# Attention scores from two products over interleaved head rows in place of three, with the low parts moved by DMA

## The chip, the cores and the metric

The kernel runs on one core of one Trainium2 chip. The metric is the device time in microseconds (us) of one execution. The time before is 929.22 us, the median of three runs (926.53 to 930.88).

## The reference

Two cross-attention layers follow one another on 8192 tokens (32 batches of 256) with 320 channels, 20 heads of 16 channels each, and 77 context keys per batch. One layer is, in short:

```python
q = split_heads(x @ Wq)            # (32, 20, 256, 16)
k, v = split_heads(ctx @ Wk), split_heads(ctx @ Wv)   # (32, 20, 77, 16)
p = softmax(q @ k.T / 4)
x = merge_heads(p @ v) @ Wo + b + x
```

The second layer does the same to the output of the first, with its own weights. The object and image-prompt branches of the original have no keys here, so the text branch is all there is.

## The kernel before

**Tiling.** The work goes in 32 units `u` (`NU`), 16 for each layer. A unit is 512 tokens, which are two batches. Channels lie on the partitions in three blocks `m` of 128, 128 and 64 rows. A context unit `w` serves two units, so the projections of keys and values (`K`, `V` in the code) stand only in even units, which are therefore longer: an even and an odd unit together take about 55 us.

**Rounded products.** TensorE multiplies rounded operands (type F32R) fast, so a value is held as a rounded high part and a low remainder. Queries are `QH` and `QL`, keys `KH` and `KL`. A score is the sum of three products: `KH*QH`, `KH*QL` and `KL*QH`.

**Heads.** In a group of 32 rows lie two heads of 16 rows. The key tiles are masked, once for the first head and once for the second, so that a product over all 32 rows gives one head's scores. Four row groups `j` of 32 rows work on TensorE side by side.

**`run(u, k, n, ...)`** is the inner piece, called for k = 0 to 4 in each unit. In ten steps it issues the score matmuls of unit `u` (`keys_by_tokens`, L391), the subtraction of the row maxima (`less_maxima`, L397), and a rough set of scores of the next unit `n = u + 1` for those maxima (`tokens_by_keys`, L378). ScalarE then takes the exponential of the four PSUM banks (L763) and frees them for the next `run`. Between the runs stand, in an order written out by hand, the projections `Q`, `K`, `V` (L307, L257, L287), the output projection `out(u - 2)` (L307) and the product with the values `PV` (L444), which gives 16 output rows and one row of sums for each head. `take(..., bank, reader)` makes TensorE wait until the last reader of a PSUM bank is done; for a query projection of block m that reader is `Q_lo(u, m)`.

**VectorE** takes the maxima (L1034), makes the low parts (`Q_lo` L995, `K_lo` L958), copies PV's output from PSUM (`o_copy` L1049, writes `Oraw`), and adds bias and residual (L1101). Its order is written out by hand as well. At the end of an even unit it is: last maxima, `Q_lo(u+2, 2)`, `Q_hi(u+2, 1)` (L987), `Q_lo(u+2, 1)`, `split_o` (L1090), then `o_copy` of k = 4, 2, 3.

**SP** issues nearly all DMAs in one hand-made order, and a wait in it holds up everything that stands behind. For each unit these are: `load_x` (L1369, L1371; the second copies 64 rows into both halves of the partitions, `broadcast_to([2, 64, N])`), `values` (L1404), `sums` (L1417, L1422: the softmax sums into `Zg` and `Zt`), `natural` (L1434, L1441: 12 DMAs that merge PV's output into `On`), `put_recips` (L1448, L1451: the reciprocals to DRAM), `spread` (L1468: the reciprocals back from DRAM, each head's row repeated on 16 partitions), `store` (L1482, L1483) and, in even units, `load_c` (L1380). `load_x(u + 3)` waits until `store(u - 2)` has landed, since both use the same of five buffers `X32`. POOL multiplies `On` with the spread reciprocals (L1293) and splits it (L1300).

The order that SP follows in an even unit, after `put_recips`, is the line

```python
spread(v, 0); spread(v, 1); store(z); load_c(u // 2 + 2); sums(u, 0); load_x(u + 3)   # v = u - 1, z = u - 2
```

(written in one line here).

Of the kernel before, what the change touches and what calls it, by code (L numbers as in the profile page):

```python
# [7 lines left out]
F32 = mybir.dt.float32  # L8
# [8 lines left out]
N = 512  # L17
# [4 lines left out]
L4 = L * 4  # L22
MT = [128, 128, 64]
# [6 lines left out]
QC = 2 * N + SQ  # L30

# [3 lines left out]
def constants():  # L35
    ident = np.eye(128, dtype=np.float32)
    mask = np.zeros((128, 2), np.float32)
    for p in range(2):
        mask[(np.arange(128) // D) % 2 == p, p] = 1.0
    neg = np.zeros((128, NI), np.float32)  # L40
    for j in range(4):
        for i in range(NI):
            neg[32 * j + i, i] = -1.0
    return ident, mask, neg


def build(nc, a):
    with ExitStack() as ctx:
# [22 lines left out]
        KH = sb("KH", [128, 2, 4, 2, LK], F32R)  # L71
        KL = sb("KL", [128, 2, 4, 2, LK], F32R)
        KH2 = sb("KH2", [128, 4, LK], F32R)
        KL2 = sb("KL2", [128, 4, LK], F32R)
        Kt = sb("Kt", [128, L4])

        QH = sb("QH", [128, 2, QC], F32R)
        QL = sb("QL", [128, 2, QC], F32R)
# [3 lines left out]
        VA = sb("VA", [128, 2, 2, C + H])  # L82
# [15 lines left out]
        small = sb("small", [128, 4 * D])  # L98
        ones = small[0:L, :].rearrange("p (a d) -> p a d", a=2)
        Zt = small[96:128, :]  # L100
# [37 lines left out]
        d_va = [sem(f"d_va{i}") for i in range(2)]  # L138

# [35 lines left out]


# [26 lines left out]
        def _(pe):  # L203
# [140 lines left out]
            def run(u, k, n, first, second):  # L344
# [23 lines left out]
                if u is not None:  # L368
                    ms, p = GROUP[k]
                    if k % 2 == 0:  # L370
                        pe.wait_ge(q_lo[ms], u + 1)
                        pe.wait_ge(k_lo[ms], u // 2 + 1)

                def tokens_by_keys(t, j):

                    c0 = m * N + (b * 2 + t) * 128
                    kt = KH[32 * j:32 * j + 32, m, n % 4, b, :] if m < 2 else KH2[32 * j:32 * j + 32, n % 4, :]
                    return pe.matmul(pR[:, (second if j > 1 else first) + j % 2, t * LK:t * LK + LK],  # L378
# [3 lines left out]
                def keys_by_tokens(i, j):  # L382

                    h = i // 3
                    pp, c0 = (p, ms * N + h * SQ) if ms < 2 else (h, 2 * N)
                    Q_ = (QH, QL, QH)[i % 3]
                    if ms < 2:
                        kt = (KH, KH, KL)[i % 3][32 * j:32 * j + 32, ms, u % 4, h, :]
                    else:
                        kt = (KH2, KH2, KL2)[i % 3][32 * j:32 * j + 32, u % 4, :]  # L390
                    pe.matmul(pA[0:L, j, h * SQ:h * SQ + SQ], kt[:, pp * L:pp * L + L],  # L391
                              Q_[32 * j:32 * j + 32, u % 2, c0:c0 + SQ],
                              start=(i == 0), stop=False, skip_group_check=True)
# [6 lines left out]
                for step in range(10):  # L400
# [3 lines left out]
                    for j in (0, 1):  # L404
                        if step < 2 and n is not None:
                            f = tokens_by_keys(step, j)
                        if 2 <= step < 8 and u is not None:
                            keys_by_tokens(step - 2, j)
                        if step >= 8 and u is not None:
                            g = less_maxima(step - 8, j)  # L410
                    if n is not None and step == 1:
                        f.then_inc(x_pe, 1)
                    if u is not None and step == 9:
                        g.then_inc(s_pe, 1)

                    if n is not None and step == 8:
                        take_pair(second, 1)
                    for j in (2, 3):
                        if step < 6 and u is not None:
                            keys_by_tokens(step, j)  # L420
                        if 6 <= step < 8 and u is not None:
                            less_maxima(step - 6, j)
                        if step >= 8 and n is not None:
                            f = tokens_by_keys(step - 8, j)
                    if n is not None and step == 9:
                        f.then_inc(x_pe, 1)

            def PV(u, k, bank):
# [9 lines left out]
                for b in range(2):  # L438
                    for j in range(4):
# [4 lines left out]
                        f = pe.matmul(bank[32 * j:32 * j + D + 1, b * SQ:b * SQ + SQ], VA[0:L, u % 2, b, h:C + H:H], src,  # L444
# [3 lines left out]
            def PV_last(k, o_bank=None, z_bank=None):  # L448
# [11 lines left out]
                for what in ("OL", "ZL"):  # L460
                    bank = psum(slot[what, m])
                    for half in range(2):
                        for j in range(4):
# [8 lines left out]
                            f = pe.matmul(dst, VL[0:L, b, h:2 * C:H] if what == "OL" else ones[:, pp, :], src,  # L472
# [29 lines left out]
            pe.wait_ge(zeros, 1)  # L502
            for b in (0, 1, 2, 3, 7):
# [119 lines left out]
        def _(act):  # L623
# [27 lines left out]
            def K(w, m):  # L651
# [3 lines left out]
                first = 2 * w % 4  # L655
# [965 lines left out]
```

## Time and profile before

| | us |
|---|---|
| median of three runs | 929.22 |
| lowest, highest run | 926.53, 930.88 |
| span of the profiled execution | 926.1 |
| TensorE matmuls busy | 903.4 |
| VectorE busy | 685.7 |
| ScalarE busy | 544.6 |
| POOL busy | 402.8 |

The profiled execution has no time of its own beside its span; the span lies 0.4 us under the lowest run and 3.1 us under the median. Busy times are unions: where four small matmuls overlap, the time counts once. The "DMA share" of a window is the mean busy share of 16 DMA engines, so 0.50 is eight engines at work.

### The profile page before, as it was taken

The page shows a single profiled execution, that of the slowest core. Times are in us where ns is not written, and L with a number is a line of the kernel's source. Part 1 is how long each engine was busy: PE and PEld are TensorE (multiplying, and loading weights), DVE is VectorE, ACT ScalarE, POOL GpSimd, SP SyncE. Part 2 cuts the span into 40 slices and gives each one's busy share as a digit, 9 for nine tenths or more (in the row PEclk, how much of TensorE's full clock was granted, in tenths as well). Part 3 has the DMA queues.
Part 4 walks back from the last instruction along what each step waited for, and adds up shares of the span by engine and source line. Part 5 has one row for each costly group of instructions (what it writes and reads, how often), then busy time and mean ns, then how long its engine had stood idle before and what let it go on. Part 6 is the DMA issues. An engine that isn't in the chain of part 4 may idle for free.

```text
span 926.1 us, 28090 instructions
## 1 busy us (share of the span) xinstructions
PE 903.4 (98%) x11518; PEld 681.3 (74%) x11518; DVE 685.7 (74%) x1221; ACT 544.6 (59%) x549; POOL 402.8 (43%) x229
## 2 busy tenths in 40 slices
PE   8899999999999999999999999999999999999897
PEld 5777778777787777777777777777778777777665
DVE  3775787868778686787868688786786868678557
ACT  4456565656556556666556656556665656656553
POOL 3424263633436263366624446364344625433224
PEclk9999999999999999999999999999999999999999
DMA  6313534445444544545555444544534544443342
GB/s 203 102 32 80 138 93 132 135 124 148 98 119 119 164 131 110 149 115 140 141 148 140 102 118 113 137 132 123 134 95 118 139 131 134 102 130 78 86 134 94
DMA packets 80526, 112.41 MB, mean 121 GB/s; under 512 B 21200, under 2 KB 37878, under 8 KB 80400
## 3 DMA queue, kind: packets, MB, share of 16 engines
q1 hardware_dynamic: 80208, 110.35, 44.4%
q8 instruction: 94, 1.54, 0.8%
q10 hardware_dynamic: 192, 0.26, 0.2%
q14 instruction: 32, 0.26, 0.1%
HBM read 60.24 MB, written 22.24 MB: 89 GB/s over the span
## 4 chain that ended last, share of the span: by engine, by line
PE 82%; DVE 6%; DMA 4%; SPq 3%; issue 2%; ACT 1%; POOL 1%; DVEq 0%; ACTq 0%; POOLq 0%
PE pR L307 27%; PE pR L444 14%; PE pA L391 10%; PE pR L378 8%; PE pR L287 4%; PE pR L329 4%; PE pR L257 4%; DMA X<-in_xT 2%; PE pA L397 2%; PE pR L261 2%; DVE OS L1090 2%; SPq L1434 1%; PE pA L307 1%; DVE QL L995 1%; PE pR L244 1%
## 5 line engine op out<-in xcount | busy, mean ns | idle before, releaser
L763 ACT ACTIVATE P<-pA 77x2048 f32<-77x2048 f32 x160 | 300.4, 1878 | 197.2 <-PE pA L397 196.9
L1034 DVE TENSOR_REDUCE Mx<-pR 128x4 f32<-128x308 f32 (+1 forms) x480 | 259.2, 575 | 31.8 <-PE pR L378 26.6
L1293 POOL TENSOR_TENSOR On<-On,OS 128x1024 f32<-128x1024 f32 (+1 forms) x58 | 105.8, 1845 | 257.8 <-DMA OS<-rd 257.8
L307 PE MATMUL pR<-OS,Wo 128*128 128x512 f32 x638 | 168.1, 402 | 2.9 <-DVE OS L1090 2.1
L444 PE MATMUL pR<-P,VA 77*17 77x256 f32 x2480 | 157.4, 385 | 0.8 <-ACT P L763 0.5
L378 PEld LDWEIGHTS pR<-KH,QH 32*128 32x128 f32 x1280 | 96.3, 183 | 70.8 <-issue 46.6
L391 PE MATMUL pA<-QH,KH 32*77 32x256 f32 x1280 | 145.0, 291 | 0.1
L1258 POOL TENSOR_TENSOR XS<-X,XS 128x1024 fp32r<-128x1024 f32 x31 | 74.0, 2387 | 152.1 <-ACT XS L649 152.1
L378 PE MATMUL pR<-KH,QH 32*128 32x154 f32 x1280 | 131.5, 283 | 7.8 <-DVE X L1101 2.2
L307 PEld LDWEIGHTS pR<-OS,Wo 128*128 128x128 f32 x638 | 113.8, 188 | 33.2 <-issue 6.3
L391 PE MATMUL pA<-QL,KH 32*77 32x256 f32 x1280 | 134.9, 275 | 0.0
L391 PE MATMUL pA<-QH,KL 32*77 32x256 f32 x1280 | 134.9, 274 | 0.0
L307 PE MATMUL pR<-XS,Wq 128*128 128x512 f32 x488 | 127.3, 403 | 0.3 <-DVE Mx L1034 0.2
L444 PEld LDWEIGHTS pR<-P,VA 77*17 77x17 f32 x2480 | 72.5, 113 | 66.1 <-issue 33.2
L1101 DVE SCALAR_TENSOR_TENSOR X<-pR,bias,X 128x512 f32<-128x512 f32 (+1 forms) x92 | 68.8, 748 | 53.0 <-PE pR L307 52.7
L307 PEld LDWEIGHTS pR<-XS,Wq 128*128 128x128 f32 x488 | 87.3, 188 | 21.8 <-DVE Mx L1034 0.7
L397 PE MATMUL pA<-Mt,neg 32*77 32x256 f32 x1280 | 102.0, 277 | 0.0
L391 PEld LDWEIGHTS pA<-QL,KH 32*77 32x77 f32 x1280 | 91.2, 141 | 0.0
L391 PEld LDWEIGHTS pA<-QH,KL 32*77 32x77 f32 x1280 | 90.9, 140 | 0.0
L391 PEld LDWEIGHTS pA<-QH,KH 32*77 32x77 f32 x1280 | 83.8, 141 | 2.2 <-issue 1.6
L1300 POOL TENSOR_TENSOR OS<-On,OS 128x1024 fp32r<-128x1024 f32 x31 | 74.3, 2397 | 22.7 <-ACT OS L786 22.4
L397 PEld LDWEIGHTS pA<-Mt,neg 32*77 32x77 f32 x1280 | 77.1, 140 | 0.0
(161 smaller groups left out, 1289.6 us busy)
## 6 DMA issues: line engine op xcount, KB each, us to landing
On<-Oraw SPq DMA_DIRECT2D x244, 64.0 KB, 2.7
OS<-rd SPq DMA_DIRECT2D x58, 256.0 KB
C<-in_cT SPq DMA_DIRECT2D x16, 616.0 KB, 7.9
X<-in_xT SPq DMA_DIRECT2D x16, 512.0 KB
y<-X SPq DMA_DIRECT2D x16, 512.0 KB, 4.0
X<-y SPq DMA_DIRECT2D x16, 512.0 KB
out<-X SPq DMA_DIRECT2D x15, 512.0 KB, 4.0
X<-in_xT SPq DMA_DIRECT2D x16, 256.0 KB
```

The lines of the kernel that those rows point to most:

```text
L257: pe.matmul(p[:, 0:L4], Wk[:, k, hi:hi + 128], (CHI, CLO)[c][:, k, :], start=(k == 0 and c == 0), stop=False)
L307: f = pe.matmul(p[:, :], W[:, k, c0:c0 + 128], S[:, s, :], start=(i == 0), stop=(i == len(pairs) - 1))
L378: return pe.matmul(pR[:, (second if j > 1 else first) + j % 2, t * LK:t * LK + LK], QH[32 * j:32 * j + 32, n % 2, c0:c0 + 128], kt, start= ...
L391: pe.matmul(pA[0:L, j, h * SQ:h * SQ + SQ], kt[:, pp * L:pp * L + L], Q_[32 * j:32 * j + 32, u % 2, c0:c0 + SQ], start=(i == 0), stop=Fals ...
L397: return pe.matmul(pA[0:L, j, h * SQ:h * SQ + SQ], neg[32 * j:32 * j + 32, i:i + 1].broadcast_to([32, L]), Mt[32 * j:32 * j + 32, :], star ...
L444: f = pe.matmul(bank[32 * j:32 * j + D + 1, b * SQ:b * SQ + SQ], VA[0:L, u % 2, b, h:C + H:H], src, start=True, stop=True, skip_group_chec ...
L763: act.activation(P[0:L, i % PR, :, :], pA[0:L, :, :], ACT.Exp, scale=float(D) ** -0.5).then_inc(p_done, 1)
L1034: dve.tensor_reduce(Mx[:, :, :].rearrange("p t (j i) -> p j t i", j=4)[:, j:j + banks, :, i:i + 2], pR[:, bank:bank + banks, 0:2 * LK].rea ...
L1101: dve.scalar_tensor_tensor(out=X32[0:M, x, m, :], in0=p[0:M, :], scalar=bias[0:M, l, m:m + 1], in1=X32[0:M, x, m, :], op0=ALU.add, op1=ALU ...
L1258: pool.tensor_tensor(XS[:, 3:5, :], X32[:, x, 0:2, :], XS[:, 0:2, :].bitcast(F32), ALU.subtract).then_inc(x_lo, 1)
L1293: pool.tensor_tensor(On[rows, blocks, :], On[rows, blocks, :], recips(u, part).bitcast(F32), ALU.mult).then_inc(o_mul, 1)
L1300: pool.tensor_tensor(OS[:, 3:5, :], On[:, 0:2, :], OS[:, 0:2, :].bitcast(F32), ALU.subtract).then_inc(o_lo, 1)
```

## The change

Rows of two heads are interleaved instead of stacked: in every group of 32 rows the even rows belong to one head and the odd rows to the other (the weights are permuted for it on the host, and the mask follows). A key tile masked for one head then has free rows, and so does the query tile. `keys` copies the high keys into the free rows of the low tile `KL`. `queries_a` and `queries_b` put the low queries into the free rows: for the even head into `QH`, for the odd head into a new tile `TB`, which also gets the high queries of the odd head. Each score is then two products over 32 rows, `KH*Q` and `KL*Q`, and `run` has eight steps, not ten. `QL` and `TB` have one buffer each, not two, so `Q_lo(u, m)` waits until all query DMAs of the units before have landed. PV writes 32 rows, not 17 (16 interleaved with the sums), so that `natural` needs 4 DMAs, not 12. `spread` now fetches four heads with each DMA for the even and odd rows of two blocks (four DMAs and one for the tail, where there were two and one), and `sums` has one DMA more. `Q_lo(., 2)` stands in the next unit on VectorE.

```diff
-                for step in range(10):
+                for step in range(8):
...
             def Q_lo(u, m):
...
                 dve.wait_ge(q_hi[m][u % 2], u // 2 + 1)
+                if u:
+                    dve.wait_ge(d_tb[m], 32 * u)
                 dve.tensor_tensor(lo, q, hi.bitcast(F32), ALU.subtract).then_inc(q_lo[m], 1)
...
-                        f = pe.matmul(bank[32 * j:32 * j + D + 1, b * SQ:b * SQ + SQ], VA[0:L, u % 2, b, h:C + H:H], src,
+                        f = pe.matmul(bank[32 * j:32 * j + 32, b * SQ:b * SQ + SQ], values_and_one(u, b, h), src,
...
+            def keys(w, tail):
+                if w >= NW:
+                    return
+                for m in ((0, 1), (2,))[tail]:
+                    sp.wait_ge(k_lo[m], w + 1)
+                for p in range(2):
+                    here, there = (EVEN, ODD) if p == 0 else (ODD, EVEN)
...
+                    sp.dma_start(lo[there].bitcast(F32), hi[here].bitcast(F32)).then_inc(d_k[tail], 16)
+
+            def queries_b(u, m):
...
+                sp.wait_ge(q_hi[m][u % 2], u // 2 + 1)
+                if u:
+                    sp.wait_ge(s_pe, NG * (u - 1) + (2, 4, 5)[m])
+                sp.dma_start(TB[ODD, cols].bitcast(F32), QH[ODD, u % 2, cols].bitcast(F32)).then_inc(d_ta[m], 16)
+                sp.wait_ge(q_lo[m], u + 1)
+                sp.dma_start(TB[EVEN, cols].bitcast(F32), QL[ODD, cols].bitcast(F32)).then_inc(d_tb[m], 16)
+
+            def queries_a(u, m):
...
+                sp.wait_ge(x_pe, 2 * (NG * u + (2, 4, 5)[m]))
+                sp.wait_ge(d_ta[m], 16 * (u + 1))
+                sp.dma_start(QH[ODD, u % 2, cols].bitcast(F32), QL[EVEN, cols].bitcast(F32)).then_inc(d_tb[m], 16)
...
+                if part == 0:
+                    for m in range(2):
+                        for p in range(2):
+                            src = a["rd"][u, 8 * p * N:8 * p * N + 8 * N].rearrange("(j m o c) -> m j o c", m=2, o=1, c=N)
+                            sp.dma_start(recips(u, part)[(EVEN, ODD)[p], m, :].bitcast(F32),
+                                         src[m].broadcast_to([4, D, N])).then_inc(d_rb, 16)
...
@@ SP, even unit
                     for r in range(3):
                         natural(v, r)
+                    queries_b(n, 0)
                     put_recips(v, 0)
                     put_recips(v, 1)
+                    keys(w, 0)
+                    queries_a(n, 0)
                     spread(v, 0)
                     spread(v, 1)
                     store(z)
                     load_c(u // 2 + 2)
-                    sums(u, 0)
+                    queries_b(n, 1)
                     load_x(u + 3)
+                    queries_a(n, 1)
+                    queries_b(n, 2)
+                    keys(w, 1)
+                    queries_a(n, 2)
@@ SP, odd unit
                     values(u + 1)
+                    queries_b(n, 1)
                     spread(v, 0)
                     spread(v, 1)
+                    queries_a(n, 1)
                     store(z)
                     sums(u, 0)
+                    queries_b(n, 2)
+                    queries_a(n, 2)
```

## Rows read from the trace of the kernel before

**Rows 1.** The page, busy time by engine (us, share of span, instructions).

```profile
PE 903.4 (98%) x11518; PEld 681.3 (74%) x11518; DVE 685.7 (74%) x1221; ACT 544.6 (59%) x549; POOL 402.8 (43%) x229
```

**Rows 2.** Groups of instructions on the page: busy us, mean ns, idle before.

```profile
L444 PE MATMUL pR<-P,VA 77*17 77x256 f32 x2480 | 157.4, 385 | 0.8 <-ACT P L763 0.5
L391 PE MATMUL pA<-QL,KH 32*77 32x256 f32 x1280 | 134.9, 275 | 0.0
...
L391 PEld LDWEIGHTS pA<-QL,KH 32*77 32x77 f32 x1280 | 91.2, 141 | 0.0
```

**Rows 3.** Timeline of TensorE in one run: start us, us, instruction.

```profile
402.96 0.28 PE L391 MATMUL pA<-QH,KH 32*77 32x256 f32 x2
...
403.55 0.27 PE L391 MATMUL pA<-QH,KL 32*77 32x256 f32 x2
```

**Rows 4.** PV by tile and in the last unit's timeline: ns min/median/max, starts.

```profile
L444 PEld LDWEIGHTS pR<-P,VA x2480: 107/109/155, 56.0 to 889.1; 77*17 77x17 f32 x191
...
L472 PEld LDWEIGHTS pR<-P,small x64: 110/110/110, 897.7 to 908.9; 77*32 77x32 f32 x64
...
897.02 1.10 PE L472 MATMUL pR<-P,CS 77*32 77x256 f32 x16
897.94 1.05 PE L472 MATMUL pR<-P,small 77*32 77x256 f32 x16
```

**Rows 5.** Timeline of SP's DMA issues in even unit 22 and after.

```profile
643.98 0.37 SPq L1369 DMA_DIRECT2D X<-y  x1
...
657.15 0.58 SPq L1448 DMA_DIRECT2D rd<-Zg  x1
...
659.81 1.92 SPq L1468 DMA_DIRECT2D OS<-rd  x3
...
662.27 0.55 SPq L1483 DMA_DIRECT2D out<-X  x1
...
668.34 0.59 SPq L1417 DMA_DIRECT2D Zg<-Oraw  x1
669.59 0.36 SPq L1369 DMA_DIRECT2D X<-y  x1
670.00 0.54 SPq L1371 DMA_DIRECT2D X<-y  x1
675.56 0.57 SPq L1422 DMA_DIRECT2D small<-Oraw  x1
```

**Rows 6.** Waits in total: us, times, longest; SP's own and one of VectorE.

```profile
SPq L1369 <- DMA y<-X: 16.0, 11, 2.6
...
DVE small L1061 <- DMA small<-Oraw: 5.6, 11, 1.0
```

**Rows 7.** Windows: busy us (x instructions) of PE, PEld, DVE, ACT, POOL, clock, DMA share, GB/s.

```profile
636.50:637.50 1.00, 1.00 (x37) 0.89 (x29) 0.97 (x3) 0.34 (x1) 0.00 (x0) 1.00 0.50 184
673.50:677.50 4.00, 3.97 (x85) 2.64 (x74) 3.97 (x7) 0.32 (x1) 3.92 (x4) 1.00 0.13 41
```

**Rows 8.** Timeline of VectorE at the end of even unit 22.

```profile
671.79 0.69 DVE L995 TENSOR_TENSOR QL<-pR,QH 128x512 fp32r<-128x512 f32 x1
672.51 2.30 DVE L1090 TENSOR_TENSOR OS<-On,OS 64x512 fp32r<-64x512 f32 x1
674.84 1.89 DVE L1049 COPY Oraw<-pR 128x512 f32<-128x512 f32 x3
...
679.24 0.55 DVE L1061 RECIPROCAL small<-small 32x64 f32<-32x64 f32 x1 [1.03 <-DMA small<-Oraw]
```

**Rows 9.** Timeline of TensorE in the same stretch.

```profile
672.88 2.80 PE L444 MATMUL pR<-P,VA 77*17 77x256 f32 x48
675.68 0.34 PE L378 MATMUL pR<-KH,QH 32*128 32x154 f32 x2
```

**Rows 10.** Windows around TensorE's two pauses in unit 30.

```profile
872.00:876.00 4.00, 2.73 (x46) 1.98 (x44) 2.77 (x7) 1.47 (x2) 0.00 (x0) 1.00 0.01 2
876.00:880.00 4.00, 3.24 (x17) 1.80 (x21) 0.96 (x2) 2.17 (x2) 0.00 (x0) 0.62 0.50 84
```

More of the change, by code:

```diff
@@ L22 @@
 L4 = L * 4
+LP = L + 1
 MT = [128, 128, 64]
@@ L30 @@
 QC = 2 * N + SQ
+OSLOT = (0, 2, 1, 3, 4)
+HH = H // 2
+HPOS = [HH * (1 - h % 2) + h // 2 for h in range(16)] + [18, 19, 8, 9]
 WORDER = ["Wk0", "Wq0", "Wv0", "Wo0", "Wk1", "Wv1", "Wq1", "Wo1"]
@@ L138, in build @@
         d_va = [sem(f"d_va{i}") for i in range(2)]
+        d_k = [sem(f"d_k{i}") for i in range(2)]
+        d_ta = [sem(f"d_ta{m}") for m in range(3)]
+        d_tb = [sem(f"d_tb{m}") for m in range(3)]
         d_zg, d_rw, d_rb = (sem(f"d_{n}") for n in ("zg", "rw", "rb"))
@@ L471, in PV_last @@
                                 first = half == 0
-                            f = pe.matmul(dst, VL[0:L, b, h:2 * C:H] if what == "OL" else ones[:, pp, :], src,
+                            g, vl = HPOS[h], VL[0:L, b, :]
+                            if what == "ZL":
+                                lhs = stripes[:, pp:pp + 32] if m < 2 else blocks[:, D * pp:D * pp + 32]
+                            else:
+                                lhs = columns(vl, g, H)
+                            f = pe.matmul(dst, lhs, src,
                                           start=first, stop=True, skip_group_check=True)
@@ L1116, in _ @@
             maxima(0, 0, 0, 1, 2)
+            Q_lo(0, 0)
             K_hi(0, 2)
@@ L1400, in values @@
                         if u < NU - 1:
-                            src, dst = VS[row:row + rows, t, :], VA[done:done + rows, half, b, 0:C]
+                            src, dst = VS[row:row + rows, t, :], VA[done:done + rows, half, b, HH:HH + C]
                         else:
@@ L1498, in _ @@
             weight_load("Wo", 0)
+            keys(0, 0)
+            queries_b(0, 0)
+            queries_a(0, 0)
             values(0)
+            queries_b(0, 1)
+            queries_a(0, 1)
+            queries_b(0, 2)
+            queries_a(0, 2)
             for u in range(NU):
-                v, z = u - 1, u - 2
+                n, v, z, w = u + 1, u - 1, u - 2, u // 2 + 1
                 if u % 2 == 0:
@@ L1521, in _ @@
                         natural(v, r)
+                    queries_b(n, 0)
                     put_recips(v, 0)
                     put_recips(v, 1)
+                    keys(w, 0)
+                    queries_a(n, 0)
                     spread(v, 0)
```

216 lines of the change are left out of this document (123 added, 93 removed).

## The prediction

> **What bounds the kernel now.** The page comes first: TensorE is busy for 903.4 of 926.1 us and VectorE for 685.7 [rows 1], so the order of TensorE's work is the time, and no other engine has a claim of its own. The waits come next. TensorE has hardly any, but SP has one to keep in mind: 11 times `load_x` waited for a store into DRAM to land, and VectorE waited as often for a small DMA [rows 6]. The timelines of an even unit, SP's, VectorE's and TensorE's, then show how closely the pieces follow one another: `Q_lo(u+2, 1)` ends at 672.48, and the PV product whose bank it frees begins about 673.8, the second third of the PV row [rows 8, 9]. The reader should see in them that the kernel lives on slack of one or two microseconds. What the change takes from TensorE is therefore easy to price. What it hangs between SP and `Q_lo` is what decides.
>
> **Part 1, a third of the score products goes.** From the first full step of a run to its last, five steps take 403.55 - 402.96 = 0.59 us [rows 3], so 0.118 us each; four matmuls run side by side, and 1280 of them are removed [rows 2]. Two steps fewer in each of 160 runs give 160 x 0.236 = -37.8 us, or -1.18 us for each unit. Every one lies on TensorE, the bound, so this gain is real as long as nobody is late. `tokens_by_keys` grows from 154 to 156 columns: below 1 ns per matmul, nothing.
>
> **Part 2, PV with 32 columns.** The last unit has such matmuls already. A set of 16 follows the other after 897.94 - 897.02 = 0.92 us, and its weight load takes 110 ns where 17 columns take 109 [rows 4]; three sets of 17 columns take 2.80 us, 0.93 each [rows 9]. I take nothing. The Trainium skill (TensorE: Matmul & The Clock Gate, section "LDWEIGHTS (loading the stationary operand)") says that a load takes its columns divided by 1.2 in ns. By that 15 more columns would be 12.5 ns, an estimate, times 2480 loads, 31 us if each were exposed; the row contradicts it here, 110 against 109 ns.
>
> **Part 3, how a DMA is spread over engines.** This gets the longest look, since the change adds 9 query DMAs to a unit and 4 key DMAs to a pair, and takes away 8 `natural` ones. SP issues them at about 0.63 us each (1.92 for three [rows 5]): -5.0 us for `natural`, +5.7 for queries, +1.3 for two keys, +1.3 for two more `spread`, +0.6 for `sums`, so SP is some 4 us busier in a unit of 27, which it can bear.
>
> The engines are another matter. While only the first two `spread` DMAs run (source: 8 heads, each repeated), the DMA share is 0.50: eight engines [rows 7]. When only the second part of `load_x` runs (source: 2 copies), it is 0.13: two engines [rows 7]. So the outermost count of a broadcast source is the number of engines. The new `spread` DMAs have 4 heads in the source, hence four engines. The first eight move 184 GB/s in 2 KB rows, 0.089 us for a row on an engine; 256 rows over eight are 2.85 us, over four 5.7 us. The reciprocals and all that queues behind them on those four come **2.85 us later**. The bound below is nothing, if the DMAs went to different engines, but in the row both earlier ones share the same eight.
>
> The Trainium skill (DMA: Bandwidth & Descriptors, section "Why a DMA increments its semaphore by 16 and not by 1") says the same: the number of engines, at most 16, is the largest that divides the slowest dimension of both sides. By that rule the new DMAs get 4 as well, and the trace's 8 and 2 agree.
>
> An engine works off its DMAs in order. The small `Zt` transfer issued at 675.56 reaches VectorE only at 679.24, when the X broadcast issued at 670.00 is through [rows 5, 8]. So that broadcast takes 9.0 us from its issue, and **whatever SP issues behind it lands no sooner**.
>
> **Part 4, the new wait on VectorE.** `QL` has one buffer now. `Q_lo(u+2, 1)` at the end of even unit `u` must wait for `queries_a(u+1, 1)` to land. On SP that stands right behind `load_x(u+3)`, which waits for `store(u-2)`, which stands behind `spread`. Added up on the clock of unit 22:
>
> - the first `spread` DMA is at 659.81 before [rows 5]. TensorE is 0.5 us ahead by then and `natural` no longer delays `put_recips`, but two key and three query DMAs stand ahead: 659.2.
> - two more issues make the second `store` DMA come 3.7 us later, not 2.46: 662.9.
> - it landed 7.3 us after issue (662.27, then `load_x` at 669.59 [rows 5]), and comes 2.85 us later: 673.1.
> - `load_x` is issued at once, its broadcast lands 0.4 + 9.0 us later: 682.5, and `queries_a` with it, 682.8.
>
> `Q_lo(u+2, 1)` was at 671.79 [rows 8] and would now be due at 670.6. It is held for 12.2 us. Behind it on VectorE stand `split_o` and all three `o_copy`; TensorE waits for it at the second PV set, after 1.35 us of slack, and gets to the next unit 10.8 us late. In unit 22 `load_x` waited 0.7 us for the store (SP was free at 668.93 [rows 5]), and in some units not at all (11 waits [rows 6]), so a store can land in 6.6 us or less; with 6.2 us, and no loss from four engines, it is 12.2 - 1.1 - 2.85 = 8.2 us held and 6.9 us lost. I take 11.5, not 10.8, since `load_x(u+2)` at the top of the unit is held likewise, and so are the sums issued behind it.
>
> **Part 5, the other end.** In an odd unit `queries_a(n, 2)` can only be issued when `queries_b(n, 2)` has landed, behind `spread` and `store`. Before, that store landed at 643.98 [rows 5]; now some 2 us later, and 2.2 us more for the second DMA: 648.2. `Q_lo(u+1, 2)`, moved to the front of the even unit on VectorE, wants it at 644.7, and `split_o`, two `K_lo` and `Q_lo(u+1, 1)` queue behind, for which TensorE waits. After 1.2 us of slack this costs 2.3 us. The bounds are 0 and 3.
>
> **Part 6, the clock.** In unit 30 TensorE was busy for only 2.73 of 4 us, and the granted clock then fell to 0.62 on average over the next window, part of it at 1.2 GHz and not 2.4 [rows 10]. A pause of 10 us is far deeper. The fall in that row covers about 3 us ((1 - 0.62) x 4 / 0.5), half of which is lost time; the bounds are 0 and 3.4 us for each pause, and I take 2.
>
> **The sum.** For a pair of units: -2.36 + 11.5 + 2.3 + 2 = +13.4 us. The wait exists in even units 2 to 28, 14 of them: +188. The other 20 runs still save 4.7. From the span of 926.1 this makes 1109; the runs shown have their median 3.1 above that span, so 1112, rounded to **1110 us**.
>
> **Rivals.**
> *The chain holds, but the links are shorter* (spreads don't lose by four engines, the store lands early, the clock stays up). For: in some units `load_x` did not wait at all. Pair: -2.36 + 6.9 = +4.5 to about +9: 985 to 1055 us. Chance 0.25.
> *The queries land in time*, because they pass the X broadcast on other engines; then only part 1 counts, with perhaps 1 us lost per pair: 895 to 910 us, faster. It decides at one point: `queries_a(u+1, 1)` must land by 672.0, while `load_x` was not even issued before 669.59, so it has 2.4 us where `Zt` took 3.7 five microseconds further on. Chance 0.08.
> *The queries are in time, but the reciprocals are not*: 2.85 us later, POOL, `split_o` and `o_copy` shift by 1 to 2 us at each end of a pair, which eats the 2.36 us: 920 to 940 us. Against it: the two lateness terms rest on the same engines. Chance 0.04.
> *PV is bound by its loads*, a mechanism of its own: its 2480 loads grow from 17 to 32 columns and are no longer hidden. A load of 77 columns takes 141 ns [rows 2] and one of 17 takes 109 [rows 4], 0.53 ns a column; 15 more, all exposed, are 8 ns x 2480 = 20 us on top of the sum: 1130 us. The rule of the Trainium skill's page TensorE: Matmul & The Clock Gate would ask for it. Against it stand the 110 ns and 0.92 us of rows 4. Chance 0.03.
>
> My forecast, 1060 to 1165 us, has 0.60.
>
> **Range and chances.** The range runs from the lowest end of the short chain, 985, to 1165, where the upper bounds of parts 4 to 6 are all taken nearly (17 us per pair). That holds 0.88 less the tails, about 0.83. A measurement of this kernel can tell 0.5%, or 5 us, from no change: faster 0.09, within 0.03, slower 0.88.
>
> **What would show it.** Right: in the page of the changed kernel, TensorE's busy share falls to about 80%; the line of `Q_lo` on VectorE shows idle time of about 12 us, 14 times, released by a DMA into `QH`; between two PV sets of each even unit TensorE pauses for 10 us, and the granted clock is below 1 right after. L391 has 2560 matmuls at the same 275 ns. PV's loads stay near 110 ns. A window inside `spread` shows a DMA share near 0.25. Wrong: if `Q_lo` follows `Q_hi` without a gap in even units, part 4 falls, and with it the sign of the forecast; if the gap is there but 7 us long, the engines or the store were mis-sized.

## The result and the profile after

The changed kernel takes 1189.6 us, the median of four runs (1187.6 to 1195.9), beside 930.05 us for the kernel before on the same chip: a ratio of 1.279 with an interval of 1.274 to 1.285. The forecast of 1110 us had the direction and the place of the loss, and was 80 us short, outside its range.

The page of the changed kernel (busy time; TensorE's granted clock in 40 slices; the chain that ended last), to be held against [rows 1]:

```profile
PE 966.8 (82%) x10238; PEld 717.4 (61%) x10238; DVE 674.0 (57%) x1221; ACT 545.5 (46%) x557; POOL 394.7 (33%) x233
...
PEclk9989899897988979989798897989889799897988
...
DMA 43%; PE 30%; SPq 18%; issue 5%; DVE 2%; ACT 1%; POOL 1%; DVEq 0%; ACTq 0%; POOLq 0%
DMA TB<-QH 19%; DMA QH<-QL 10%; PE pR L324 9%; PE pR L471 7%; DMA X<-in_xT 5%; PE pR L396 5%; DMA X<-y 3%; SPq L1544 3%; PE pA L409 3%; DMA Zg<-Oraw 3%; SPq L1444 3%; PE pR L346 2%; SPq L1480 2%; SPq L1497 1%; SPq L1562 1%
```

The line of the chain on the page of the kernel before:

```profile
PE 82%; DVE 6%; DMA 4%; SPq 3%; issue 2%; ACT 1%; POOL 1%; DVEq 0%; ACTq 0%; POOLq 0%
```

TensorE has 1280 matmuls fewer than in [rows 1] and is nevertheless busy for 63 us longer, at a mean clock of 0.893. Its share of the chain fell from 82% to 30%. DMAs and SP's issues are 61% of it, and the two query transfers, into `TB` and into `QH`, 29%.

The waits, in total, number and longest (L1032 is `Q_lo`, L471 PV, L396 the rough scores, L1092 the reciprocals of the sums, L1479 the wait of `queries_a` on SP):

```profile
DVE QL L1032 <- DMA QH<-QL: 188.0, 29, 10.6
PE pR L471 <- DVE QL L1032: 120.8, 15, 9.2
...
PE pR L396 <- DVE VS L1055: 34.6, 14, 4.0
...
DVE Zg L1092 <- DMA Zg<-Oraw: 34.0, 14, 3.9
...
SPq L1479 <- DMA TB<-QH: 181.6, 48, 6.5
```

The timelines of one even unit, SP's issues first, then `Q_lo` on VectorE and TensorE's stretch between two PV sets (start, length, instruction, idle before). They answer to [rows 5, 8, 9]:

```profile
633.53 0.56 SPq L1561 DMA_DIRECT2D y<-X  x1
634.13 0.52 SPq L1562 DMA_DIRECT2D y<-X  x1
634.69 0.71 SPq L1420 DMA_DIRECT2D C<-in_cT  x1
636.40 0.51 SPq L1469 DMA_DIRECT2D TB<-QH  x1
636.96 0.67 SPq L1471 DMA_DIRECT2D TB<-QL  x1
643.29 0.37 SPq L1409 DMA_DIRECT2D X<-y  x1
643.71 0.58 SPq L1411 DMA_DIRECT2D X<-y  x1
645.32 0.49 SPq L1480 DMA_DIRECT2D QH<-QL  x1
...
652.76 0.69 DVE L1032 TENSOR_TENSOR QL<-pR,QH 128x512 fp32r<-128x512 f32 x1 [8.88 <-DMA QH<-QL]
...
644.72 1.10 PE L471 MATMUL pR<-P,VA 77*32 77x256 f32 x16
653.60 3.65 PE L471 MATMUL pR<-P,VA 77*32 77x256 f32 x32 [7.78 <-DVE QL L1032]
```

This is the chain that the prediction drew. `load_x` follows the store's second DMA by 9.2 us (643.29 - 634.13), the query DMA stands behind it, and it lands only when the broadcast is through, 7.4 us after its issue. `Q_lo` stands idle for 8.9 us. One link was not drawn: the DMA into `TB`, issued at 636.40, landed only when SP could go on at 645.3, so `queries_a` was due no earlier even without `load_x`. Ahead of it on the queue stand the spread, the store and also `load_c` (616 KB, issued at 634.69). The view of the DMAs from 625 to 660 has their time from issue to landing:

```profile
C<-in_cT SPq DMA_DIRECT2D x1, 616.0 KB, 10.2
...
TB<-QH SPq DMA_DIRECT2D x1, 128.0 KB, 8.8
```

How much of the 8.8 us is due to `load_c` was not tried; no run moves it.

Windows around the pause (busy of PE, PEld, DVE, ACT, POOL; clock; DMA share; GB/s):

```profile
644.00:648.00 4.00, 1.82 (x22) 1.08 (x21) 0.00 (x0) 1.10 (x3) 3.92 (x4) 1.00 0.69 215
648.00:652.00 4.00, 0.00 (x0) 0.00 (x0) 0.00 (x0) 0.00 (x0) 2.66 (x1) 0.81 0.22 78
652.00:656.00 4.00, 2.40 (x24) 1.38 (x28) 2.47 (x4) 0.00 (x0) 0.00 (x0) 0.50 0.08 27
656.00:660.00 4.00, 4.00 (x46) 2.74 (x39) 2.52 (x5) 0.79 (x1) 0.00 (x0) 0.50 0.11 29
660.00:664.00 4.00, 4.00 (x42) 2.98 (x42) 3.02 (x8) 3.19 (x3) 1.46 (x1) 0.91 0.30 117
```

TensorE's granted clock falls during the pause and stays at 0.50, its lower level of 1.2 GHz, for the next 8 us. That is longer than the 3 us that [rows 10] suggested, after a longer pause. The two PV sets behind the pause take 3.65 us there, and 1.97 to 2.19 us elsewhere in this trace.

### The profile page after: what moved, and what is told of

The parts are those of the page before. It is cut to its first block, busy times and chain, and to the rows that moved or that the text cites. A ratio compares the mean times of both kernels' runs of the same rounds, so it can differ in the third digit from the quotient of the medians.

```text
span 1185.6 us, 26038 instructions
## 1 busy us (share of the span) xinstructions
PE 966.8 (82%) x10238; PEld 717.4 (61%) x10238; DVE 674.0 (57%) x1221; ACT 545.5 (46%) x557; POOL 394.7 (33%) x233
## 4 chain that ended last, share of the span: by engine, by line
DMA 43%; PE 30%; SPq 18%; issue 5%; DVE 2%; ACT 1%; POOL 1%; DVEq 0%; ACTq 0%; POOLq 0%
DMA TB<-QH 19%; DMA QH<-QL 10%; PE pR L324 9%; PE pR L471 7%; DMA X<-in_xT 5%; PE pR L396 5%; DMA X<-y 3%; SPq L1544 3%; PE pA L409 3%; DMA Zg<-Oraw 3%; SPq L1444 3%; PE pR L346 2%; SPq L1480 2%; SPq L1497 1%; SPq L1562 1%
## 5 line engine op out<-in xcount | busy, mean ns | idle before, releaser
L471 PE MATMUL pR<-P,VA 77*32 77x256 f32 x2480 | 189.8, 440 | 121.5 <-DVE QL L1032 120.8
L324 PE MATMUL pR<-OS,Wo 128*128 128x512 f32 x638 | 196.1, 453 | 32.7 <-DVE OS L1127 29.9
L471 PEld LDWEIGHTS pR<-P,VA 77*32 77x32 f32 x2480 | 95.6, 148 | 192.1 <-issue 178.0
L396 PE MATMUL pR<-KH,QH 32*128 32x156 f32 x1280 | 147.9, 310 | 45.7 <-DVE VS L1055 34.6
L396 PEld LDWEIGHTS pR<-KH,QH 32*128 32x128 f32 x1280 | 105.6, 198 | 120.6 <-issue 65.3
L1032 DVE TENSOR_TENSOR QL<-pR,QH 128x512 fp32r<-128x512 f32 x61 | 42.0, 689 | 180.1 <-DMA QH<-QL 137.6
L1138 DVE SCALAR_TENSOR_TENSOR X<-pR,bias,X 128x512 f32<-128x512 f32 (+1 forms) x92 | 68.5, 746 | 66.7 <-PE pR L324 66.7
L824 ACT ACTIVATE OS<-On 128x1024 fp32r<-128x1024 f32 (+1 forms) x62 | 52.1, 842 | 73.9 <-POOL On L1329 73.9
L409 PE MATMUL pA<-QH,KH 32*77 32x256 f32 x640 | 76.4, 321 | 0.1
L1086 DVE COPY Oraw<-pR 128x512 f32<-128x512 f32 x78 | 53.7, 689 | 30.9 <-PE pR L471 30.5
L409 PE MATMUL pA<-QH,KL 32*77 32x256 f32 x640 | 70.0, 300 | 0.0
L814 ACT ACTIVATE Oraw<-pR 128x512 f32<-128x512 f32 x77 | 46.1, 598 | 50.2 <-PE pR L471 50.2
```

What stands on the lines that cost most here:

```text
L324: f = pe.matmul(p[:, :], W[:, k, c0:c0 + 128], S[:, s, :], start=(i == 0), stop=(i == len(pairs) - 1))
L409: pe.matmul(pA[0:L, j, h * SQ:h * SQ + SQ], kt, q, start=(i == 0), stop=False, skip_group_check=True)
L471: f = pe.matmul(bank[32 * j:32 * j + 32, b * SQ:b * SQ + SQ], values_and_one(u, b, h), src, start=True, stop=True, skip_group_check=True)
L1086: dve.tensor_copy(Oraw[:, OSLOT[k], :], psum(slot["PV", u, k])[:, :]).then_inc(o_raw[k][u % 2], 1)
L1138: dve.scalar_tensor_tensor(out=X32[0:M, x, m, :], in0=p[0:M, :], scalar=bias[0:M, l, m:m + 1], in1=X32[0:M, x, m, :], op0=ALU.add, op1=ALU ...
```

## The experiments

Times are medians. "Before" was 930 to 932 us beside each of them, the changed kernel 1190 us.

### The order, X, and the spread, one at a time

`e1`: `queries_a` ahead of `load_x`.

```diff
-                    load_x(u + 3)
                     queries_a(n, 1)
+                    load_x(u + 3)
                     queries_b(n, 2)
```

> Edit: in even units SP issues queries_a(n, 1) ahead of load_x(u+3), not behind it; all else as in the changed kernel. Theory (the pause is the DMA into QH queued behind the X broadcast on its two engines): in the even unit at 645 the DMA into QH was issued at 645.3 and landed at 652.7, 7.4 us, against a median of 3.5 us for such DMAs; ahead of X it should take about 3.5, so the pause shrinks by some 4 us in 15 pairs: 1190 - 60 = 1130 us, Q_lo's longest idle 5 us instead of 10.6. Rival (the pause hangs on the earlier DMA into TB, which lands 8.8 us after its issue behind spread and store; what follows it does not matter): no change beyond 10 us, 1180 to 1195. Rival (load_x(u+3), now some 2.6 us later, is itself on a closed chain and hands the delay on): above 1190.

Measured: 1162.6 us, ratio 1.247 [1.242, 1.253]. In between the theories. SP's timeline, and `Q_lo`:

```profile
632.00 0.47 SPq L1480 DMA_DIRECT2D QH<-QL  x1
632.59 0.51 SPq L1409 DMA_DIRECT2D X<-y  x1
633.14 0.58 SPq L1411 DMA_DIRECT2D X<-y  x1
633.82 0.49 SPq L1469 DMA_DIRECT2D TB<-QH  x1
634.67 0.48 SPq L1471 DMA_DIRECT2D TB<-QL  x1
635.21 1.23 SPq L1459 DMA_DIRECT2D KL<-KH  x2
641.96 0.46 SPq L1480 DMA_DIRECT2D QH<-QL  x1
...
634.09 0.69 DVE L1032 TENSOR_TENSOR QL<-pR,QH 128x512 fp32r<-128x512 f32 x1 [3.44 <-DMA QH<-QL]
```

The query DMA now lands 2.1 us after its issue (634.09 - 632.00), so the link was real. But the next DMA into `TB`, at 633.82, has come behind the broadcast, and SP waits for it until 641.96 before it can issue the following one. That wait on SP (L1479) grew from 181.6 to 283.7 us in total. Of these 102 us, 77 only stand where `load_x` waited for the store before (46.5 and 30.4 us there, none here). TensorE's wait for `Q_lo` fell from 120.8 to 36.2 us, but its wait for the residual on VectorE (L1138) grew from 1.9 to 52.4 us. Of the 4 us for a pair that the theory had, more than half did not come.

`e2`: the broadcast split.

```diff
-                sp.dma_start(X32[:, x, 2, :],
-                             src[256:C, cols].rearrange("(h p) n -> h p n", h=1).broadcast_to([2, 64, N])).then_inc(d_x[x], 16)
+                for h in range(2):
+                    sp.dma_start(X32[64 * h:64 * h + 64, x, 2, :], src[256:C, cols]).then_inc(d_x[x], 16)
```

> Edit: the second part of load_x, one DMA with a source of 2 copies of 64 rows, becomes two DMAs of 64 rows each, everywhere; all else as in the changed kernel. Theory (two engines carry the broadcast for 9 us, and whatever has a row on them waits): the DMA into QH lands 3.5 us after its issue and not 7.4, the sums DMA no longer waits 3.9 us behind it, and the transfers of X are through in about 3 us: 6 to 8 us less for a pair, 1070 to 1100 us. Rival (the spread DMAs on four engines and the store are what holds the DMA into TB): 3 us less for a pair at most, 1145 to 1175. Rival (SP is the bound, one more issue of 0.6 us for each load): 1190 to 1200.

Measured: 1094.6 us, ratio 1.174 [1.169, 1.179]. The theory held in time. The second part of `load_x` lands 4.2 us after its issue at the median, SP's wait for `TB` fell from 181.6 to 109.0 us, TensorE's for `Q_lo` from 120.8 to 74.9, and VectorE's for the DMA into `Zg` from 34.0 us to 1.1. The broadcast on two engines cost the changed kernel 95 us by what queued behind it.

`e3` leaves out the score DMAs, the calls of `keys`, `queries_a` and `queries_b`.

```diff
-                        pe.wait_ge(d_tb[ms], 32 * (u + 1))
-                        pe.wait_ge(d_k[ms // 2], 32 * (u // 2 + 1))
+                        pe.wait_ge(q_lo[ms], u + 1)
+                        pe.wait_ge(k_lo[ms], u // 2 + 1)
...
-                if u:
-                    dve.wait_ge(d_tb[m], 32 * u)
```

> Edit: the changed kernel without the DMAs keys, queries_a and queries_b and without the waits for them (TensorE waits for Q_lo and K_lo instead, and reads QH for both heads); it leaves out the low parts of the queries and of the high keys' partner, so its scores lack these terms. What is left of the change is two score products, PV of 32 columns, four natural DMAs and the spread of four heads each. Theory (part 1 real, PV's columns free): 930 - 37.8 = 892 us, and up to 10 more by the late reciprocals. Rival (PV bound by its loads of 32 columns): 20 us more, 912 or above. Rival (the spread on four engines alone costs 1 to 2 us at each end of a pair): 915 to 940 us.

Measured: 1005.2 us, ratio 1.081 [1.074, 1.087], above all three. So the score DMAs and the waits for them are 184 of the 260 us, and the remaining 75 had to be explained by something else.

`e4` puts one part of that something into the kernel before.

```diff
+                    for q in range(MT[m] // 64):
+                        src = a["rd"][u, (8 * m + 4 * q) * N:(8 * m + 4 * q + 4) * N].rearrange("(h o c) -> h o c", o=1, c=N)
+                        sp.dma_start(recips(u, part)[64 * q:64 * q + 64, m % 2, :].bitcast(F32),
+                                     src.broadcast_to([4, D, N])).then_inc((d_rb, d_rbt)[part], 16)
```

> Edit: the kernel before with its spread DMAs of 8 heads split into DMAs of 4 heads each (four and one, as the changed kernel has them, in contiguous rows); nothing else. Theory (engines used = number of heads in the source): the reciprocals land 2.85 us later and SP is busy 1.3 us more for a unit; TensorE has slack of 1 to 2 us, so 930 to 955 us, with a DMA share near 0.25 while they run. Rival (the DMAs take different engines): share 0.5, 928 to 932 us.

Measured: 999.7 us, ratio 1.070 [1.061, 1.079]. Same bytes, same rows, some 65 us more by the ratio, 57 to 74 by its interval. A window while only these DMAs run:

```profile
412.00:413.00 1.00, 1.00 (x37) 0.89 (x29) 0.87 (x4) 0.37 (x1) 0.00 (x0) 1.00 0.26 96
```

and the page's line of busy times:

```profile
PE 937.3 (93%) x11518; PEld 701.6 (70%) x11518; DVE 710.8 (71%) x1221; ACT 546.7 (54%) x549; POOL 401.8 (40%) x229
```

The share is 0.26, four engines, where [rows 7] show 0.50. The mechanism of part 3 held, and I had not seen how much it could cost by itself: 65 us over 31 units is 2.1 us a unit, beside 2.85 us of delay. The slack of one or two microseconds takes little of it. The profiled execution is the longest of the four, 79 us above [rows 1] in its span: 34 us of that show as TensorE's busy time at a mean clock of 0.960, and 45 us as its idle time. The 65 us are not the engines' alone, since the edit also has two more issues on SP for each unit. `e5` and `e7` below add an issue and still gain 51 and 59 us from eight engines, so the engines are the larger part.

`e5` and `e6` give the changed kernel's spreads more engines. The edit shown is that of `e5`; `e6` stores the reciprocals four times and takes `broadcast_to([16, 4, N])`.

```diff
-                    sp.dma_start(a["rd"][u, 0:16 * N].rearrange("(i c) -> i c", c=64), Zg[:, :]).then_inc(d_rw, 16)
+                    rd = a["rd"][u, 0:16 * 2 * N].rearrange("(q d i c) -> d q i c", q=8, d=2, c=64)
+                    for d in range(2):
+                        sp.dma_start(rd[d], Zg[:, :]).then_inc(d_rw, 16)
...
-                                         src[m].broadcast_to([4, D, N])).then_inc(d_rb, 16)
+                                         src[m].broadcast_to([8, 8, N])).then_inc(d_rb, 16)
```

> Edit: the changed kernel, with put_recips storing the reciprocals twice into DRAM (one more DMA), so that the source of each spread DMA is 8 rows of which each goes to 8 partitions, not 4 rows for 16 each; same bytes. Theory (the spread on four engines costs the same here as alone, 68 us there; SP pays 0.6 us for the second store of reciprocals): 1190 - 55 = 1135 us, between 1120 and 1150, and a higher DMA share while the spreads run. Rival (in the changed kernel the X broadcast and the closed chain through load_x hide it): 1175 to 1195.

> Edit: as the one with 8 engines, but the reciprocals are stored four times (three DMAs more) and each spread source is 16 rows for 4 partitions each. Theory (bytes per engine count): 1.4 us faster again for each spread, but SP pays 1.3 us more for each; the same as with 8 engines within 10 us. Rival (engines are all): 30 us below the one with 8. Rival (SP is a link of the chain now): 15 to 40 us above it.

Measured: 1138.6 us (ratio 1.221 [1.214, 1.228]) and 1139.0 us (1.224 [1.219, 1.229]). Both as the theories had it: 51 us from eight engines, and nothing more from sixteen at the price of two more issues. What sixteen engines give without these issues was not tried.

`e7` is `e3` with eight engines, `e12` the same with X split as well, and `e8` the changed kernel with the edits of `e1`, `e2` and `e5` together.

> Edit: the changed kernel without keys, queries_a, queries_b and their waits (the scores lack the low parts' terms, as before) and with the reciprocals stored twice, so that the spreads use 8 engines. Theory (what kept that kernel at 1005 us and not at 892 is the spread on four engines, which costs more when TensorE is faster): 892 to 905 us. Rival (the order of sums and natural, or PV's 32 columns, cost as well): 925 to 960.

Measured: 946.3 us, ratio 1.017 [1.012, 1.022]. The spread is 59 us here. But 54 us are left above 892, so the theory fell and the rival held.

> Edit: the changed kernel without keys, queries_a, queries_b and their waits, with spread sources of 8 rows and the X broadcast as two DMAs. It was at 946 us with the spread alone. Theory (what is left above the kernel before are late reciprocals behind X's two engines): 915 to 930. Rival (the order of SP's pieces, sums in the odd unit and two more spread DMAs): 935 to 948, no change from the X edit.

Measured: 936.8 us, ratio 1.010 [1.006, 1.013]. That lies in the rival's range, but the X edit did change something: 9.5 us by the medians, 7 by the ratios (1.017 and 1.010).

> Edit: the changed kernel with three repairs together: queries_a(n, 1) ahead of load_x(u+3) in even units, the X broadcast as two DMAs, the spread sources of 8 rows. Theory (each link's delay adds up: 95 us for X, 27 for the order, of which half is the same delay, and 55 for the spread): 1025 us, between 1000 and 1050. Rival (after two links a third takes over, SP's own issue time or the store that load_x waits for): 1060 to 1090.

Measured: 1019.1 us, ratio 1.093 [1.089, 1.098]. The delays add up: one at a time the three gave 27, 95 and 51 us, together 171. Repaired in three places the change still costs 89 us.

`e11` gives the repairs of X and the spread (sixteen engines) to the kernel before.

> Edit: the kernel before with the X broadcast as two DMAs of 64 rows, and the reciprocals stored twice so that each spread source is 16 rows; nothing else. Theory (TensorE's order is the time, the DMAs have slack): within 5 us of before, 925 to 932. Rival (SP's two more issues for each unit hold something up): 935 to 950. Rival (transfers were late in places): 915 to 922.

Measured: 943.5 us, ratio 1.016 [1.013, 1.018]. Faster transfers, and 14 us slower. What the edit adds besides is two issues on SP for each unit, 1.3 us, and the rival that rests on them had 935 to 950. That they are the cause is argued and not shown: the edit also puts the spread on sixteen engines, where it can stand in the way of other transfers, and the two were not taken apart. TensorE has a new wait in it, 16.1 us in 11 places for VectorE's maxima (L1034).

### The clock

`e10`: matmuls nobody reads, ahead of the PV set that waits.

```diff
                     PV(u, 4, 3)
+                    if u:
+                        p = take(("spent",), 2)
+                        kh = KH[:, 0, n // 2 % 2, :, :, :, :].rearrange("p a s b k -> p (a s b k)")
+                        for i in range(28):
+                            pe.matmul(p[:, :], kh[:, 0:128], kh[:, 0:N], start=True, stop=True)
                     PV(u, 2, 1)
```

> Edit: the changed kernel with 28 matmuls that nobody reads (7.3 us) on TensorE in each even unit from 2 on, between the first PV set and the one that waits for Q_lo; results unchanged. Theory (the clock's fall after each pause is lost time on the bound, 8.5 us at half speed in the even unit at 652, so some 4 us for each of 14 pairs): 1190 - 56 = 1134 us, mean clock 0.97 or more, the PV sets behind the pause 2.0 us and not 3.65. Rival (what closes the loop is SP and the DMAs; TensorE only waits longer when it is faster): clock up likewise, time 1175 to 1195, and the idle of TensorE grows by what its matmuls gained.

Measured: 1156.3 us, ratio 1.245 [1.241, 1.249]. TensorE with the pause filled:

```profile
212.58 1.96 PE L471 MATMUL pR<-P,VA 77*32 77x256 f32 x32 [1.37 <-DVE QL L1037]
...
622.83 6.64 PE L617 MATMUL pR<-KH 128*128 128x512 f32 x28 [0.32 <-ACT Mt L794]
631.37 2.59 PE L471 MATMUL pR<-P,VA 77*32 77x256 f32 x32 [1.90 <-DVE QL L1037]
```

The sets behind it take 1.96 to 2.05 us in most of the 14 filled pauses (2.59 in the one at 631, 3.03 at most) and not 3.65, the mean clock is 0.945 and not 0.893, and the time is 33 us lower, 2.4 us for each filled pause. Part 6 had taken 2. The rest of the theory's 56 us was not there. It fits the rival's loop of SP and DMAs, which closes at nearly the same time: VectorE still waits 184.0 us for the DMA into `QH`, where it was 188.0.

### Why a third of the products gives nothing

`e9` is the kernel before with `KH*QL` left out, and eight steps.

```diff
-                    Q_ = (QH, QL, QH)[i % 3]
+                    Q_ = (QH, QH)[i % 2]
...
-                for step in range(10):
+                for step in range(8):
```

> Edit: the kernel before with one score product of three left out (KH with QL), so that run has eight steps and not ten; its scores lack that term, and nothing else differs. Part 1 of the prediction alone (0.236 us for each of 160 runs): 892 us. Rival, from the changed kernel's traces: a run at full clock takes 1.26 us there against 1.33 to 1.40 before, 0.07 to 0.14 less and not 0.236, since the second pair of the rough score products starts 0.22 and not 0.12 us after the last maxima products: 908 to 919 us.

Measured: 924.6 us, ratio 0.993 [0.991, 0.996]. Even less than the rival said: 5 us, with 11 us less busy time. The next three ask why. `e13` and `e14` halve the exponential, `e15` puts the second pair of rough products ahead of the last maxima products.

> Edit: the kernel before with ScalarE's exponential over two of the four score banks only (from the fourth on), so it leaves out half of the probabilities and takes about 0.95 us instead of 1.88. It is the control for the next one. Theory (TensorE's own order is the time in the kernel before): 920 to 932 us. Rival (the loop last maxima product, exponential, next run is what paces, 3.43 us a round): 30 us or more below before.

> Edit: the kernel before with two steps fewer in each run (KH with QL left out) and the exponential over two banks of four. Theory (with two steps fewer TensorE waits for the exponential, which is 1.88 us long and hides only behind 2.1 us of other work): without that wait part 1 shows, 890 to 900 us. Rival (the steps themselves give only 0.07 to 0.14 us a run back, whatever ScalarE does): at most 5 us under the same two steps with the full exponential, 915 to 925.

Measured: 926.8 us (ratio 0.996 [0.992, 1.000]) and 920.5 us (0.990 [0.986, 0.994]). Half an exponential gives 4 to 5 us with ten steps and with eight, so it is not what hides the two steps.

> Edit: the kernel before with two steps fewer, and in its last two steps the second pair of rough score products (with the wait for its banks) goes ahead of the last maxima products, not behind them. Theory (the 0.10 us that opened ahead of that pair is TensorE's own queue coming to the wait late, with fewer products issued ahead): the gap moves to the new place ahead of the pair and stays 0.2 us; time within 4 us of 925. Rival (the gap belongs to the pair's place behind four maxima products): it closes to 0.12 us, 905 to 915 us. Rival (the last maxima products come later, the exponential with them): 930 or above.

Measured: 926.4 us, ratio 0.995 [0.993, 0.998]. The gap went where the pair went: the pair starts 0.88 us after the run at the median, in `e15` as in `e9`. One of its runs, whose PV sets stand just ahead of it:

```profile
402.74 0.28 PE L397 MATMUL pA<-Mt,neg 32*77 32x256 f32 x2
403.19 0.34 PE L378 MATMUL pR<-KH,QH 32*128 32x154 f32 x2 [0.17 <-DVE Oraw L1057]
403.19 0.34 PE L397 MATMUL pA<-Mt,neg 32*77 32x256 f32 x2
```

So the gap belongs to the pair's wait, whose banks `take_pair` takes. Who frees them? `e9`, TensorE in a run that starts at 403.45, and VectorE beside it:

```profile
404.11 0.38 PE L397 MATMUL pA<-Mt,neg 32*77 32x256 f32 x4
404.36 0.34 PE L378 MATMUL pR<-KH,QH 32*128 32x154 f32 x2
...
403.56 0.75 DVE L1101 SCALAR_TENSOR_TENSOR X<-pR,bias,X 128x512 f32<-128x512 f32 x1 [0.79 <-PE pR L307]
```

The same of the kernel before, in a run that starts at 402.68:

```profile
403.57 0.37 PE L397 MATMUL pA<-Mt,neg 32*77 32x256 f32 x4
403.69 0.34 PE L378 MATMUL pR<-KH,QH 32*128 32x154 f32 x2
...
402.79 0.75 DVE L1101 SCALAR_TENSOR_TENSOR X<-pR,bias,X 128x512 f32<-128x512 f32 x1 [0.58 <-PE pR L307]
```

The pair writes into the bank that held the output projection just ahead of the run. VectorE has read it out 0.86 us after the run starts in both. With ten steps the pair comes after 1.01 us, with eight it would come after 0.77, and waits until 0.91. `e16` and `e17` halve these copies, with ten and with eight steps.

```diff
-                dve.tensor_copy(Oraw[:, k, :], psum(slot["PV", u, k])[:, :])
+                c = N if u < 2 else SQ
+                dve.tensor_copy(Oraw[:, k, 0:c], psum(slot["PV", u, k])[:, 0:c])
```

(the same on ScalarE and for the bias and residual)

> Edit: the kernel before, but the copies that free the PSUM banks of PV and of the output projection take 256 columns of 512 (o_copy on ScalarE and VectorE, the bias and residual on VectorE; from the third unit on for o_copy), so half of the output is left out. Control for the next one. In the kernel before the second pair of rough products comes 1.01 us after a run's start, later than the copies end, so both theories expect little: 920 to 931 us, a run 1.33 to 1.40 us as before.

> Edit: as the control, and two score steps fewer in each run (KH with QL left out). Theory (with eight steps the second pair is due 0.77 us after the run's start, but its bank holds the output of the piece ahead of the run, whose copy is through only after 0.9 us: 404.31 for a pair that starts at 404.36): with half copies the pair is no longer held, a run takes 1.1 to 1.2 us at the median and not 1.27, and the time is 10 to 20 us under its control, 900 to 912 us. Rival (TensorE's own queue makes the gap): the gap stays 0.22 us, and the time is within 8 us of its control.

Measured: 922.1 us (ratio 0.990 [0.986, 0.994]) and 908.6 us (0.974 [0.970, 0.978]). `e17`, in a run that starts at 394.94:

```profile
395.60 0.38 PE L397 MATMUL pA<-Mt,neg 32*77 32x256 f32 x4
395.71 0.34 PE L378 MATMUL pR<-KH,QH 32*128 32x154 f32 x4
...
395.05 0.48 DVE L1103 SCALAR_TENSOR_TENSOR X<-pR,bias,X 128x256 f32<-128x256 f32 x1 [0.79 <-PE pR L307]
```

The copy is through after 0.59 us, the pair follows without a gap, and a run takes 1.13 us at the median of 155, against 1.27 in `e9`, 1.33 in the kernel before and 1.32 in the control. In the changed kernel it is 1.26 us. Two steps fewer are worth 13.6 us here and 5 with full copies. The wait is shown as the reason for a part, some 8 to 9 us. For the rest, some 24 us, the profiled executions say where it lies: TensorE's busy time fell by 25.8 us of 37.8 (900.1 to 874.3), and its idle time grew by 14 (22.0 to 36.1). Whose slack these are was not tried.

## Why the prediction was wrong where it was

The terms, in the prediction's order, with what the experiments make of them:

| part | predicted, us | measured, us | from |
|---|---|---|---|
| 1, two steps fewer | -37.8 | -5 | `e9` |
| 2 and SP's added work | 0 | +22 | `e7` less `e9` |
| 3, spread on four engines | in 4 to 6 | +59 | `e3` less `e7` |
| 4 to 6, score DMAs, waits, clock | +221 with part 3 | +184 (with part 3: +243) | after less `e3` |
| sum | +183 | +260 | |

The measured column is one path from the kernel before to the changed one, with one thing added at a time. Another order would share the 260 us out otherwise: the spread alone is 65 us in the kernel before, 59 without the score DMAs and 51 in the changed kernel.

**Part 1 is the step that failed.** "Every one lies on TensorE, the bound, so this gain is real as long as nobody is late." The 0.118 us for a step was read rightly, but from the inside of a run [rows 3], and then given to the whole of it. In the run's last part somebody is late: the copy that frees the second pair's bank. Its slack was 0.15 us (1.01 - 0.86), less than the 0.236 us taken away, and no wait list shows a slack before it is used up. The error is 33 us; with -5 in its place the sum is 1143 us, inside the range. The copy accounts for some 8 or 9 of the 33, as far as the runs show, and the cause of the rest stays open.

**Part 2 held**, and the rival from its loads fell. Three PV sets in a row take 2.83 us (in `e7`; the changed kernel's trace has no three in a row) against 2.80 [rows 9], and a single set 1.10 against 1.07, so 155 sets cost at most some 5 us, although a load takes 140 ns at the median against 109 [rows 4]:

```profile
L471 PEld LDWEIGHTS pR<-P,VA x2480: 132/140/181, 59.6 to 1140.3; 77*32 77x32 f32 x191
```

The 110 ns that I relied on [rows 4] belong to a constant operand, the ones that give the softmax sums, in 32 adjacent columns. The values in the same stretch of the kernel before, 32 columns at a stride of 20, show the slower load:

```profile
L472 PEld LDWEIGHTS pR<-P,CS x64: 135/138/161, 897.0 to 908.0; 77*32 77x32 f32 x64
```

The load grew by 31 ns, far more than the trace's 0.53 ns a column gives for 15 columns (8 ns), but with matmuls of 379 ns beside it nearly all of it stays hidden. The rule of the Trainium skill (TensorE: Matmul & The Clock Gate, section "LDWEIGHTS (loading the stationary operand)") gives 12.5 ns for these columns, an estimate; the trace has 31, and the measurement decides.

**Part 3 was right** on engines (0.26 in `e4`, and by the rule of the Trainium skill's page DMA: Bandwidth & Descriptors, section "Why a DMA increments its semaphore by 16 and not by 1", the trace agrees) and on what queues behind. Its sentence "SP is some 4 us busier in a unit of 27, which it can bear" has no run behind it, and two runs speak against it. `e11` lost 14 us with 1.3 us more of issues in a unit, and `e7` is 22 us above `e9` with at most 5 us from PV. Of the 22, 7 to 9.5 us go with X's two engines (`e12`). How the rest divides between SP's order, the later `sums` and PV was not taken apart.

**Parts 4 and 5** had the mechanism and the place. `Q_lo` was idle for 8.9 us in the unit shown and 10.6 at most, where 12.2 were expected. The store landed 9.2 us after issue and not 10.1. `load_x` was issued at once and the queries landed 9.5 us after it (652.76 - 643.29), as expected. TensorE lost 8.4 us on average in the 14 waits that I had counted, where I took 11.5: 117 us in all and not 161. A fifteenth wait, in unit 0, adds 3.5 us. At the other end `Q_lo(u+1, 2)` was held for 3.6 us on average (50 us in 14 pairs), where part 5 had 3.5 (648.2 - 644.7). Too small was the allowance for the sums behind `load_x(u + 2)`, 0.7 us for a pair (11.5 less 10.8): VectorE waited 34.0 us in 14 pairs for the DMA into `Zg`, and 1.1 us, once, in `e2`, and TensorE waited 34.6 us behind it (L396), 2.5 us for a pair. That SP itself waits for the DMA into `TB` (181.6 us) was in the sum only at the odd end; it is a wait of the new code on a queue that carries everything.

**Part 6** had the size of one pause (2.4 against 2 us), but not all that the clock takes. TensorE is busy for 966.8 us in the changed kernel and for 892.0 in `e9`, which has as many matmuls. Filling the pauses gave back some 29 of these 75 us (1031.2 us in `e10`, of which the fillers are about 93), and the clock was still 0.945 on average. Up to 5 us of the other 46 are PV's wider sets. How much of them lies on the path was not tried.

That parts 3 to 6 together came within 22 us (+221 and +243) is therefore partly luck: the main wait was taken 44 us too large, and the sums' wait and the clock too small.

Of the signs that I named, the busy share (82%), the clock and the spread's share (0.26 in `e4`) came as said. The idle `Q_lo` (8.9 us, for 12) and the pause between the PV sets (7.8 us, for 10) came in kind, and shorter. L391's matmuls (now L409) did not keep 275 ns, but have a mean of 277 to 321 ns in four groups, some of them at the lower clock, and PV's loads did not stay at 110.

The rival whose time came nearest was that of PV's loads, 1130 us, by a mechanism that the trace contradicts.

## What to carry to other kernels

A gain measured inside a tight piece of code is only as large as the slack of whoever frees its buffers: before shortening a piece, take the time from its start to the last PSUM bank it claims, and the time to the end of the copy that frees that bank, and let no more than the difference count. That is an upper bound. Here the difference, 0.15 us in 160 runs, is 24 us, and 5 came.

Of every DMA that repeats a source, read from the DMA share of a window how many engines it uses, and of everything issued behind it on the same queue, how long it waits. Four heads in place of eight cost 51 to 65 us, with not one byte more. A DMA that waits for an earlier DMA's landing is better kept off a queue that also issues the loads; that is read from the 181.6 us of SP's wait, and a second queue was not tried.

## What the runs showed of the hardware

- Sixteen engines for the spread gave nothing over eight (1139.0 against 1138.6 us, with two more issues for each unit), although eight gave 51 us over four.
- After a pause of 7.8 us TensorE's granted clock was 0.50 (1.2 GHz of 2.4) for two windows of 4 us, in which it was busy for 2.4 and 4.0 us; after [rows 10]'s shorter pause it was 0.62 on average over one.
- A weight load of 32 columns took 140 ns at the median at a stride of ten values, 138 at a stride of 20 and 110 where the columns are adjacent; 17 columns at a stride of 20 took 109 [rows 4].
